# A scan over tokens shared by five engines: GpSimd makes every third drive product, TensorE's gaps are filled, transfers are moved

## The reference

```python
u = silu(conv(x_branch) + conv_b)                    # [B, 384, 192]
dt = softplus(u @ dt_w.T + dt_b)
Bv = u @ B_w.T ; Cv = u @ C_w.T                      # [B, 384, 16]
dA = exp(dt[..., None] * A)                          # A: [192, 16]
dBu = dt[..., None] * Bv[:, :, None, :] * u[..., None]
h = dA_t * h + dBu_t                                 # over the 384 tokens
y_t = einsum('bdn,bn->bd', h, C_t)
y = (y + D_param * u) * silu(z) ; r = y @ out_w.T + residual
h = h + layernorm(r) ; h = h + experts(layernorm(h)) # 8 experts, the best 2 of each token
```

## Time and profile before

| what | value |
|---|---|
| median of 3 runs | 445.19 us (444.76 to 445.53) |
| the profiled execution's own time | 445.39 us |
| its span in the profile | 443.6 us |
| mean granted share of TensorE's clock | 0.933 |
| busy: PE, DVE, ACT, POOL | 84%, 62%, 45%, 53% of the span |
| first scan of step 0 starts, last scan of step 47 starts | 72.0 us, 230.5 us |
| experts' tiles | from about 288 us to the end |

### The profile page before, as it was taken

The page is one execution under the profiler, slowest core; times in us unless marked ns, Lnnn a source line. Parts: engine busy times, 40 slices in busy tenths (PEclk is TensorE's granted clock), DMA queues, the critical chain, the costliest instruction groups (busy, mean ns, idle before and its releaser), DMA issues.

```text
span 443.6 us, 6744 instructions
## 1 busy us (share of the span) xinstructions
PE 373.6 (84%) x2265; PEld 280.8 (63%) x2265; DVE 274.4 (62%) x470; ACT 197.9 (45%) x502; POOL 233.7 (53%) x171
## 2 busy tenths in 40 slices
PE   5889897999748958698777795899999999999970
PEld 4445654554424625354445574799999999999970
DVE  4525479898999999979992569244434343443400
ACT  1456576576824575535650220044443544444440
POOL 6877733567456737656462005334655556565431
PEclk9999997899969989989699877699999999999996
DMA  6310014453537756857374530422232322323224
GB/s 186 65 12 4 7 33 135 118 120 104 161 79 224 210 170 176 254 169 230 126 218 176 201 108 0 131 44 48 52 55 48 50 53 45 59 41 53 39 28 115
DMA packets 36038, 46.01 MB, mean 104 GB/s; under 512 B 8813, under 2 KB 25022, under 8 KB 35438
## 3 DMA queue, kind: packets, MB, share of 16 engines
q1 hardware_dynamic: 28686, 38.00, 28.8%
q0 software_dynamic: 7328, 7.71, 11.1%
HBM read 39.69 MB, written 7.18 MB: 106 GB/s over the span
## 4 chain that ended last, share of the span: by engine, by line
PE 40%; DVE 20%; issue 14%; POOL 12%; DMA 4%; SPq 4%; ACT 2%; POOLq 0%; DVEq 0%; ACTq 0%
PE ps L1073 15%; PE ps L1056 9%; DVE w_all L1585 7%; POOL w_all L577 6%; PE ps L1062 6%; DVE ps L1577 4%; POOL w_all L627 4%; PE ps L1032 2%; SPq L502 2%; DVE y_cm L1531 2%; DVE y_cm L1503 2%; PE ps L1046 2%; PE ps L887 1%; DVE stats L1440 1%; DMA b_wide_sb<-bc_dram 1%
## 5 line engine op out<-in xcount | busy, mean ns | idle before, releaser
L627 POOL TENSOR_TENSOR w_all<-w_all 128x768 f32<-128x768 f32 x48 | 80.5, 1681 | 75.2 <-DVE w_all L1585 32.2
L660 POOL DMA_INDIRECT sum_dram<-u_cm,tok_row x31 | 50.6, 1632 | 60.1 <-ACT u_cm L1406 50.3
L887 PE MATMUL ps<-w_all,cst 128*128 128x512 f32 x96 | 57.3, 681 | 21.8 <-POOL w_all L627 21.6
L1585 DVE TENSOR_TENSOR_SCAN w_all<-decay,ps 128x780 f32<-128x780 f32 x40 | 71.1, 1779 | 1.5 <-POOL w_all L627 0.2
L577 POOL DMA_INDIRECT w_all<-in_pix,gidx x42 | 45.7, 1089 | 14.7 <-issue 12.5
L1391 ACT ACTIVATE u_cm<-ps,x_cm 128x128 f32<-128x128 f32 x96 | 26.6, 377 | 54.5 <-PE ps L1062 54.5
L645 POOL DMA_INDIRECT dt_cm<-x_dram,tok_in x31 | 31.2, 1007 | 19.3 <-DVE gate_s L1750 10.1
L1577 DVE TENSOR_TENSOR ps<-dtu_cm,ps 128x768 f32<-128x768 f32 x40 | 37.9, 948 | 4.6 <-ACT ps L1306 2.8
L823 PE MATMUL ps<-cst 128*128 128x256 f32 x128 | 35.1, 429 | 5.3 <-DMA cst<-in_cst 5.3
L887 PEld LDWEIGHTS ps<-w_all,cst 128*128 128x128 f32 x96 | 17.2, 205 | 33.5 <-POOL w_all L627 29.1
L1763 DVE COPY x_cm<-w_all 128x1154 f32 x16 | 12.2, 762 | 40.2 <-PE ps L1073 40.2
(11 more groups left out here) (229 smaller groups left out, 696.4 us busy)
## 6 DMA issues: line engine op xcount, KB each, us to landing
w_all<-bc_dram SPq DMA_DIRECT2D x48, 256.0 KB, 3.4
w_all<-bc_dram SPq DMA_DIRECT2D x96, 64.0 KB, 3.5
w_all<-in_w_all SPq DMA_DIRECT2D x16, 289.0 KB, 4.1
w_all<-in_w_all SPq DMA_DIRECT2D x4, 1156.0 KB, 6.2
b_wide_sb<-bc_dram SPq DMA_DIRECT2D x8, 256.0 KB, 3.7
x_dram<-x_cm SPq DMA_DIRECT2D x3, 384.0 KB, 3.1
sum_dram<-h_tok SPq DMA_DIRECT2D x3, 384.0 KB, 3.5
out<-sum_dram SPq DMA_DIRECT2D x4, 288.0 KB, 3.8
```

The costliest lines, as they stand in the source:

```text
L627: nc.gpsimd.tensor_tensor(segments(hcs[at % 2]), inner(states[at % 2]), segments(c_sb[at % RING]), ALU.mult).then_inc(hc_rdy, 1)
L660: pool.indirect_dma_start(sum_dram, bass.IndirectOffsetOnAxis(ap=tok_row[:, i:i + 1].bitcast(U32), axis=0), y_out[:, i % 2, :], None, comp ...
L887: nc.tensor.matmul(sums[:, 0:4 * P], ident, hcs[at % 2][:, 0:4 * P], start=False, stop=at % S == S - 1, skip_group_check=True)
L1585: v.tensor_tensor_scan(states[p], fade, drive, 0.0, ALU.mult, ALU.add).then_inc(scanned, 1)
```

## The change

1. GpSimd makes the drive product at steps 5, 8, 11, ..., 47: 15 of 48, where it was 8. For the seven new ones (8, 14, 20, 26, 32, 38, 44) `spread_b` and VectorE's product fall away, and SyncE sends seven more rows of B. The row for step at + 3 is now sent at step at, behind the row of C.
2. The third `add_shift` moves from step 9 to step 18.
3. `send_rows` moves from s = 13 to s = 14. `load_expert` is issued at two of three steps from step 16 on (at % 3 is not 2), where it was every odd step, so the 16 quarters are out by step 39, where it was step 47.
4. More fillers on TensorE: four at step 1 ahead of `fine_level(1)`, twelve at step 15 where there was one, three at s = 2 in chunks 1 and 2 (into bank 4, after the waits that now stand in `attn_free`) where there was none, three at s = 8 where there was one.

```diff
         def by_pool(at):
-            return at % 6 == 5
+            return at > RING and at % RING == RING - 1
 
         def pool_drives(at):
-            return (at + 1) // 6
+            return max(0, (at + 1) // RING - 1)
...
             def broadcast_b(at):
-                if at >= 6:
-                    sp.wait_ge(pool_driven, pool_drives(at - 6))
+                if at >= 2 * RING:
+                    sp.wait_ge(pool_driven, pool_drives(at - RING))
...
-                if by_pool(at - RING) and at - RING + 6 < STEPS:
-                    broadcast_b(at - RING + 6)
-                if at > S and at % S == 13:
+                if by_pool(at) and at + RING < STEPS:
+                    broadcast_b(at + RING)
+                if at > S and at % S == 14:
                     send_rows(at // S - 1)
...
-                if at >= S and at % 2 and piece < PIECES * (E - LATE):
+                if at >= S and at % 3 != 2 and piece < PIECES * (E - LATE):
...
-                if at in (1, 5, 9):
-                    add_shift(at // 4)
+                if at in (1, 5, S + 2):
+                    add_shift(at // 4 if at < S else 2)
...
-                if by_pool(at + RING):
+                if by_pool(at + RING) and at + RING < STEPS:
                     pool_drive(at + RING)
...
-            def filler():
-
-                nc.tensor.matmul(ps[:, 7, 256:512], ident, cst[:, 0:256], start=False, stop=True, skip_group_check=True)
+            def filler(n=1, bank=7):
+
+                for _ in range(n):
+                    nc.tensor.matmul(ps[:, bank, 256:512], ident, cst[:, 0:256], start=False, stop=True,
+                                     skip_group_check=True)
...
                     if s == 1:
+                        filler(4)
                         fine_level(1)
...
+                    elif s == S - 1:
+                        filler(12)
...
-                    elif s not in (2, 4):
+                    elif s == 2:
+                        attn_free(n - 1)
+                        filler(3, 4)
+                    elif s == 8:
+                        filler(3)
+                    elif s != 4:
                         filler()
```

More of the change, by code:

```diff
@@ L890, in sum_states, with attn_free @@
                                  stop=at % S == S - 1, skip_group_check=True).then_inc(summed, 1)
-            def residual_rows(j):
+            def attn_free(j):
                 if j == 0:
@@ L899, in residual_rows @@
                     pe.wait_ge(logit_rdy, j)
+            def residual_rows(j):
+                attn_free(j)
                 for h in range(2):
```

## The result

The changed kernel took 441.6 us (median of 7 runs, 440.34 to 443.59) against 445.21 for the kernel before beside it (7 runs): a ratio of 0.9915, 95% interval 0.9886 to 0.9943. The gain is 3.6 us where 7.7 were forecast. The profiled execution took 441.27 us, span 439.4.

What follows compares the result with a forecast made beforehand. The prediction took the scan, mostly paced by VectorE, as where time could be gained; its terms summed to 7.9 us, from the profiled 445.39 to 437.5 us, with a range of 434.0 to 442.0 us.

Steps and rivals of the forecast that it cites:

- the rival of the clock: TensorE's clock goes its old way despite the fillers; gain only 3.8 us, total 441.6 us; chance 0.12.
- Step 8: Scan behind the convolution, without VectorE's drive product: 0 to 0.8 us, mostly given back at step 12, so 0.1 gained.
- the rule that speaks against the change: GpSimd's product slows beside VectorE instructions with two SBUF inputs; only state product 6, beside the convolution, at no cost.
- Step 43: Scan behind the layer norm's last part: 0 in the table; the next step was called plain, 0.95 us gained.
- Steps 18 to 25: Scan 20 catches up with state product 18, rows of B wait on TensorE: 0.9 us lost (0 to 1.5).
- a clock that falls at new places before a sum on the path: TensorE's clock, listed among the signs that would show the prediction wrong; no size given.
- Steps 37 to 42: Step 38, before the residual, where TensorE's out projection is late: 0.1 us gained (0 to 0.97).
- My -1.0 for SyncE: SyncE has no pause from step 30 to 39, rows of C for 31 to 35 late: 1.0 us lost (0 to 2.5).
- the rival of SyncE's pace: SyncE and the DMA engines set the pace of chunks 1 and 2: 3.4 us lost, total 440.1; chance 0.18.
- The last sum: End of the scan: row of C of step 46 sent first, no quarters left; 1.65 us gained (0.8 to 1.65).
- hidden products: Across the scan, the moved drive products are hidden and nothing changes: 445 us; chance 0.04.
- GpSimd as the bound: In plain steps GpSimd's four products for three steps, slowed beside VectorE, set the pace: about 460 us; chance 0.04.

Runs made afterwards that it cites:

- add4: The changed kernel with the second add_shift at step 4 instead of step 5; 439.09 us, ratio to before 0.9862.
- own_44: add4_11 with the drive product of step 44 left to VectorE; 477.1 us in a single run, where the kernel before took 483 to 484 us.
- old_places: The changed kernel with the transfers at their former places, send_rows at s = 13 and a quarter of weights at every odd step; 442.59 us, ratio 0.9964.
- add4_11: The changed kernel with the second add_shift at step 4 and the third at step 11; 439.54 us, ratio to before 0.9878.
- late_quarters: add4_11 with all sixteen quarters of weights sent behind the row of C of step 47, none during the scan; ratio to before 0.9843.
- split_quarters: add4_11 with chunk 1's quarters of weights kept and the last five sent after the last state product; ratio to before 0.9806.

## Why the forecast was wrong

The sign and the whole range, 434 to 442 us, came true, and so did eight of the thirteen terms of the table, within 0.2 us. But the forecast proper, 434 to 439.5 us with a chance of 0.62, was missed. That the rival of the clock had priced 441.6 us, the measured median to the digit, is luck: what it described did not happen in this trace. Five terms are off, and hold the difference:

1. *Step 8 and the rule that speaks against the change.* The failed step of the mechanism is the sentence that state product 6 "costs nothing on the path" because step 8 needs it 5 us later. It asked what the slower product does to GpSimd and never what it does to VectorE, which was on the path: VectorE's instruction went from 0.47 to 1.81 us. The sum had 0.1, the trace -1.06; add4 gave 1.35 back by removing the overlap alone, and its lead over these steps then changes by 0.3, near what was forecast. I had also taken over half of the sentence in the Trainium skill (GPSIMD Engine Reference, "8. Key points"): it names VectorE's instructions with two SBUF inputs and those in a two-port mode. The instruction that was hit has one input. The Trainium skill (VectorE: DVE Perf Modes, "🔬 Walkthrough: the 8-slice pipeline in each mode") says that such a product of fp32 reads its one tensor through both ports; the trace fits, with 0.47 us for it and 0.77 for the one with two inputs, over the same 524 elements. Both kinds were slowed here, by 1.34 and 1.43 us.
2. *Step 43*, the same mechanism, 0.48 us: I had taken step 44 as plain. own_44 shows it.
3. *Steps 18 to 25.* The mechanism was named (scan 20 catches up with state product 18, rows of B stand behind sums on TensorE) and mis-sized: -0.9 forecast, -2.8 measured. "Part is hidden" was not worked out: the addition ends at 139.06, 1.5 us after TensorE had released state product 18. And the fall of the clock while TensorE idled for it had no price in the sum; the text had it only as a sign of being wrong ("a clock that falls at new places before a sum on the path"), and that sign came. By old_places it holds about 1.9 of the 2.8 us, as much as was missing. Without the addition there (add4_11) 0.6 are lost, and without weights sent there as well (late_quarters) nothing.
4. *Steps 37 to 42.* Forecast 0.1, measured -0.67. The rows for GpSimd's step 38 were late (1.44 us of idle time on a DMA, ended at 201.07 us; the DMA share from 190 to 200 us is 0.92). My -1.0 for SyncE was right for steps 33 to 35 (-0.87) and stopped too early: between steps 30 and 38 late_quarters and split_quarters each gain 1.3 us more than the kernels with the quarters there. So the rival of SyncE's pace was partly true, at less than the 3.4 us it was given.
5. *The last sum.* 1.16 for 1.65: row 47 behind `send_rows` is the one that is late, as the text had in its bounds (0.8 to 1.65), by 1.4 us. By old_places only 0.64 of the 1.16 is due to the new order, with the reserve made there.

Together 1.16 + 0.48 + 1.9 + 0.77 + 0.49 = 4.8 us, less 0.24 gained behind the last sum and 0.8 ahead of the scan, against 7.9 - 4.1 = 3.8 between the forecast sum and the two profiled executions. The rivals of the clock (in this trace it went its new way at all three gaps; in three later traces not at the first), of the hidden products and of GpSimd as the bound are refuted by the leads at 3, 14, 26, 32 and 36 and by the mean of 1680 ns.

What of the kernel was worth the time: the fillers gave about 2.4 to 3.5 us; the seven drives by themselves nothing that was measured (0.9996), because each was paid for with a product pushed beside an instruction of VectorE's, an addition in the way, or a transfer. With those three mended the same drives are worth it: split_quarters is 1.9% faster than before (0.9758 to 0.9854), where the change was 0.85% (0.9886 to 0.9943).

## What to carry to other kernels

When work is added to a side engine, look at what its later work slides beside, and price the slowing for the engine on the path, not for the side engine; a stall shows as a longer duration, which no list of waits names. Move filler work of a side engine to where it already waits, and ask of every idle stretch of TensorE that you make longer what its clock does next. Transfers that nobody needs soon don't belong beside rows that are needed in 4 us, nor right behind the last of them on the same queue.

## What was not expected of the hardware

- VectorE's product with a constant over 128x524, of one SBUF input, took 1.81 us beside GpSimd's product and ended 0.30 us after it; over 128x192 it took 0.87 instead of 0.37 and ended some 0.1 us after GpSimd's. Both thus lost most of what was left of GpSimd's. Of three with two SBUF inputs beside an addition of GpSimd's one took 2.20 us instead of 0.77, and the addition, which had started while another of the three ran, 2.34 instead of 1.81. Scans and products with one operand in PSUM lose nothing: 1.78 and 0.95 us is the mean of 33 each.
- In the last eight runs TensorE took its instructions one at a time over some 40 us, in the profile of split_quarters from about 23 to 62 us, long before anything edited. Its timeline, where the idle time is ended by nothing that the profile shows:

```profile
49.91 0.58 PE L795 MATMUL ps<-u_cm,dw 128*128 128x250 f32 x1 [2.22 <-issue]
52.72 0.58 PE L795 MATMUL ps<-u_cm,dw 128*128 128x250 f32 x1 [2.22 <-issue]
```

In the changed kernel's profile the four of this line take 1.11 us together. The clock is at half in these runs until 73 to 80 us, and the scan starts at 106 to 114 us instead of 71 to 74. No run tells what holds the instructions back. That it is the chip is not shown either: the record has the chip number 6 for the first four runs and for the last two.
